# A Mamba-2 block with its MLP and a LoRA layer on one core: decay factors from broadcast cumulative sums in place of three f32 products

## The reference, cut to what matters

```
cs = cumsum(a)                                   # over the chunk's 128 tokens
Ldec[q, k] = exp(cs[q] - cs[k]) where k <= q, else 0
att = (C B^T) * Ldec ;  Yd = att @ (X * dt)
dec_end[k] = exp(cs[127] - cs[k])                # state handed to the next chunk
Yo = (C @ previous state) * exp(cs[q])
Y = Yd + Yo + D * X ;  y = Y * silu(z) ;  out = y @ w_out^T
```

## Time and profile before

| what | us |
|---|---|
| runs: median (lowest to highest), 3 runs | 778.89 (778.3 to 781.04) |
| the profiled execution, its own time | 783.21 |
| its span, first to last instruction | 781.5 |
| around the span | 1.7 |

### The profile page before, as it was taken

How to read it: one execution, slowest core, us unless ns; L and a number is a source line. 1 busy time by engine, 2 the same in 40 slices (tenths; PEclk the granted TensorE clock), 3 DMA queues, 4 the chain that set the end, 5 groups by cost and what they waited for, 6 DMA issues and landing times.

```text
span 781.5 us, 14105 instructions
## 1 busy us (share of the span) xinstructions
PE 746.2 (95%) x5626; PEld 533.6 (68%) x5634; DVE 513.3 (66%) x1181; ACT 342.5 (44%) x615; POOL 149.6 (19%) x201
## 2 busy tenths in 40 slices
PE   4999979989999999999999999999999999999985
PEld 3767846668666877588666877578666876667752
DVE  6798877787665757477664767467674767365356
ACT  2653766545623374235623363235633264222221
POOL 2220131105100321104200231103300241001021
PEclk8899999999999999999999999999999999999997
DMA  8970000030203120040202211050201201031001
GB/s 308 386 237 5 2 27 1 1 82 2 55 1 55 55 50 6 1 109 1 55 1 51 60 30 25 1 108 3 55 1 32 77 1 29 1 81 29 28 1 54
DMA packets 60082, 41.12 MB, mean 53 GB/s; under 512 B 45680, under 2 KB 45808, under 8 KB 60016
## 3 DMA queue, kind: packets, MB, share of 16 engines
q1 hardware_dynamic: 60016, 40.22, 18.6%
HBM read 25.01 MB, written 4.19 MB: 37 GB/s over the span
## 4 chain that ended last, share of the span: by engine, by line
PE 84%; DVE 8%; ACT 3%; DMA 2%; issue 1%; SPq 1%; POOL 0%; ACTq 0%; DVEq 0%
PE gu L1447 35%; PE wa L1447 24%; PE acc L1447 18%; PE wc L1447 6%; DVE xbc L1051 2%; DMA weights<-in_w_up 2%; DVE weights L973 2%; ACT weights L617 1%; DVE sg L1189 1%; DVE stats_a L1245 0%; DMA h2t<-xbc 0%; SPq L364 0%; DVE xbc L1177 0%; DVE hn L1251 0%; ACT sg L751 0%
## 5 line engine op out<-in xcount | busy, mean ns | idle before, releaser
L1447 PE MATMUL gu<-h2t,weights 128*128 128x256 f16 x2688 | 312.1, 273 | 1.9 <-DVE h2t L1183 1.0
L1447 PEld LDWEIGHTS gu<-h2t,weights 128*128 128x128 f16 x2688 | 261.9, 98 | 52.1 <-issue 10.3
L1447 PE MATMUL acc<-weights,act 128*128 128x512 f16 x672 | 163.4, 379 | 4.9 <-DVE act L1194 4.9
L1189 DVE SCALAR_TENSOR_TENSOR sg<-gu,bound,sg 128x256 f32<-128x256 f32 x112 | 53.2, 475 | 102.2 <-ACT sg L751 101.4
L751 ACT ACTIVATE sg<-gu,scale_inv 128x256 f32<-128x256 f32 x112 | 53.0, 473 | 146.5 <-PE gu L1447 146.3
L1447 PE MATMUL wa<-ht,weights 128*128 128x256 f16 x912 | 107.3, 275 | 1.3 <-DMA ht<-ra 1.1
L1447 PEld LDWEIGHTS acc<-weights,act 128*128 128x128 f16 x672 | 65.2, 98 | 62.2 <-DVE act L1194 6.9
L1447 PEld LDWEIGHTS wa<-ht,weights 128*128 128x128 f16 x912 | 90.0, 99 | 19.1 <-DMA ht<-ra 1.6
L761 ACT ACTIVATE act<-sg 128x256 f16<-128x256 f32 x112 | 46.6, 416 | 101.0 <-DVE sg L1189 101.0
L1194 DVE TENSOR_TENSOR act<-sg,act 128x256 f16<-128x256 f32 x112 | 49.8, 445 | 54.0 <-ACT act L761 54.0
L1051 DVE SCALAR_TENSOR_TENSOR xbc<-wa,conv_ws,xbc 128x253 f32<-128x253 f32 (+1 forms) x132 | 57.3, 476 | 1.8 <-ACT xbc L664 0.2
(11 more groups left out here) (233 smaller groups left out, 872.6 us busy)
## 6 DMA issues: line engine op xcount, KB each, us to landing
xa<-in_x SPq DMA_DIRECT2D x9, 512.0 KB, 3.6
weights<-in_x SPq DMA_DIRECT2D x7, 512.0 KB, 3.9
out_x<-h SPq DMA_DIRECT2D x14, 256.0 KB, 2.2
weights<-in_w_in SPq DMA_DIRECT2D x5, 512.0 KB, 6.5
weights<-in_w_down SPq DMA_DIRECT2D x3, 768.0 KB, 13.2
weights<-in_w_gate SPq DMA_DIRECT2D x2, 1024.0 KB, 13.6
weights<-in_w_up SPq DMA_DIRECT2D x2, 1024.0 KB, 14.0
weights<-in_w_gate SPq DMA_DIRECT2D x2, 768.0 KB, 14.4
```

The lines of the kernel that those rows point to most:

```text
L1189: nc.vector.scalar_tensor_tensor(sg[:, f % 2], GU[f % 2][:, SEQ:2 * SEQ], up_to_act, sg[:, f % 2], ALU.mult, ALU.mult).then_inc(sem("prod_ ...
L1447: return nc.tensor.matmul(dst, left, right, start=start, stop=stop)
```

## The change

Group 0 keeps the old way. For groups 1 to 7:

- GpSimd no longer spreads a_t over ra, TensorE no longer makes the three products.
- TensorE `a_cs`, at the end of slot 3: a_t (8 columns as the stationary side) by tri gives the cumulative sums as rows, [8, 128], and tri by a_t gives them as columns, [128, 8], both in the bank WC. ScalarE `a_cs` copies both to SBUF, in slot 3 ahead of the third Silu.
- SyncE `a_cs`, first in its step: eight DMAs, each reading one partition's row of 128 floats (512 bytes) 128 times and writing it to all partitions of ra.
- VectorE `a_fall`: for each chunk and head, a tensor_scalar that subtracts the column and takes the minimum with 0; chunk 0 in slot 4, behind a wait for all eight DMAs, chunk 1 in slot 5. The minimum bounds the entries above the diagonal, which the later product with tdt masks.
- ScalarE takes all three Exp in slot 5, in place (dec, and ra[:, 1] for ce).
- `a_h0` moves from slot 3 to slot 5, behind the second differences; SyncE's `a_x` moves behind `c_t3`. `a_state` moves from slot 6 to slot 7 on TensorE and ScalarE. TensorE's `c_logits` waits for the copied columns, because it writes the same bank.

```diff
+        cs_row = sb("cs_row", [TILES * H, P])
+        cs_col = sb("cs_col", [P, TILES, H])
...
+        cs_col_ps, cs_row_ps = WC[:, TILES * H:2 * TILES * H], WC[0:TILES * H, P:2 * P]
...
+            def a_cs(g):
+
+                sp.wait_ge(sem("cs_row_ready"), g)
+                for n in range(TILES * H):
+                    sp.dma_start(ra[:, n // H, n % H], cs_row[n:n + 1].unsqueeze(1).broadcast_to([1, P, P])).then_inc(cs_loaded, 16)
...
                 following = a is not None and a + 1 < GROUPS
-                if following:
-                    a_x(a + 1)
+                if a is not None:
+                    a_cs(a)
                 if c is not None and not alone(c):
                     c_t3(c)
                 if following:
+                    a_x(a + 1)
                     a_t1(a + 1)
...
                     a_xd(a)
-                    a_scan_in(a)
                     a_tdt(a)
...
+                eng.wait_ge(sem("fall_ready"), (g - 1) * TILES * H + H * (min(n, 1) + 1))
+                nc.scalar.activation(dst, dst, ACT.Exp).then_inc(sem("exp_ready"), 1)
+
+            def a_cs(g):
+
+                eng.wait_ge(sem("cs_ps_ready"), g)
+                nc.scalar.activation(cs_row[:], cs_row_ps, ACT.Copy).then_inc(sem("cs_row_ready"), 1)
+                nc.scalar.activation(cs_col[:].rearrange("p t h -> p (t h)"), cs_col_ps, ACT.Copy)\
+                    .then_inc(sem("cs_col_ready"), 1)
...
-                    3: lambda g: (a_silu(g, 2), a_z(g, 1)),
-                    4: lambda g: (a_tok(g), a_exp(g, 0), a_exp(g, 1)), 6: lambda g: (a_exp(g, 2), a_state(g)),
+                    3: lambda g: (a_cs(g), a_silu(g, 2), a_z(g, 1)), 4: lambda g: a_tok(g),
+                    5: lambda g: (a_exp(g, 0), a_exp(g, 1), a_exp(g, 2)), 7: lambda g: a_state(g),
...
+            def a_fall(g, j):
+
+                if j == 0:
+                    dve.wait_ge(cs_loaded, g * TILES * H * 16)
+                    dve.wait_ge(sem("cs_col_ready"), g)
+                    prev(g, 2, 2, dve, sem("y_ps_ready"))
+                for h in range(H):
+
+                    nc.vector.tensor_scalar(dec[:, j, h], ra[:, j, h], cs_col[:, j, h:h + 1], 0.0, ALU.subtract, ALU.min)\
+                        .then_inc(sem("fall_ready"), 1)
...
-                    2: lambda g: (a_conv(g, 2), a_dt(g)), 3: lambda g: a_h0(g),
-                    5: lambda g: (a_dec(g, 0), a_dec(g, 1), a_att(g, 0)), 6: lambda g: a_att(g, 1),
+                    2: lambda g: (a_conv(g, 2), a_dt(g)),
+                    4: lambda g: a_fall(g, 0), 5: lambda g: (a_fall(g, 1), a_h0(g), a_dec(g, 0), a_dec(g, 1), a_att(g, 0)), 6: lambda g: a_att(g, 1),
...
+            def a_cs(g):
+
+                pe.wait_ge(sem("a_ready"), g + 1)
+                a = a_t[:].rearrange("p t h -> p (t h)")
+                mm(cs_row_ps, a, tri[:], True, True)
+                mm(cs_col_ps, tri[:], a, True, True).then_inc(sem("cs_ps_ready"), 1)
...
-                    pe.wait_ge(sem("dtv_ready"), g + 3)
+                    pe.wait_ge(sem("cs_col_ready"), g + 2)
...
-                    3: lambda g: a_z(g, 1), 4: lambda g: (a_tok(g), a_dec(g, 0), a_dec(g, 1)),
-                    5: lambda g: (a_att(g, 0), a_dec(g, 2)), 6: lambda g: (a_att(g, 1), a_state(g)),
-                    7: lambda g: (a_y(g, 0), a_y(g, 1)), 8: lambda g: a_y_spread(g), 9: lambda g: a_o(g, 0),
+                    3: lambda g: (a_z(g, 1), a_cs(g)), 4: lambda g: a_tok(g),
+                    5: lambda g: a_att(g, 0), 6: lambda g: a_att(g, 1),
+                    7: lambda g: (a_state(g), a_y(g, 0), a_y(g, 1)), 8: lambda g: a_y_spread(g), 9: lambda g: a_o(g, 0),
```

More of the change, by code:

```diff
@@ L166, in build @@
         w0 = sb("w0", [P, H])
+        cs_row = sb("cs_row", [TILES * H, P])
+        cs_col = sb("cs_col", [P, TILES, H])
         tdt = hn[:].rearrange("p t (h q) -> p t h q", h=H)
         xw = hn[:, 0].rearrange("p (h q) -> p h q", h=H)
-        ce = hn[:, 1].rearrange("p (h q) -> p h q", h=H)
         y = sb("y", [P, H, SEQ])
@@ L289, in z_bank, with dec_bank @@
             return GU[b] if head(g) else bank(g, b)
-        def dec_bank(g, n):
-            return bank(g, [0, 1, 0][n])
+        def dec_bank(n):
+            return WA[[0, 1, 0][n]]
         def att_bank(g, j):
@@ L313, in ce_of @@
         def ce_of(g):
-            return first_ce if head(g) else ce
+            return first_ce if head(g) else ra[:, 1]
         def alone(g):
@@ L342, in build @@
         ht_loaded, h2t_loaded, h3t_loaded = sem("ht_loaded"), sem("h2t_loaded"), sem("h3t_loaded")
+        cs_loaded = sem("cs_loaded")
         masks_made = sem("masks_made")
@@ L485, in a_scan_in @@
             def a_scan_in(g):
-                pool.wait_ge(sem("a_ready"), g + 1)
+                pool.wait_ge(sem("a_ready"), 1)
                 for j in range(TILES):
-                    if j == 0:
-                        prev(g, 3, 3, pool, sem("dec_ps_ready"))
                     nc.gpsimd.tensor_tensor(ra[:, j], tri[:].unsqueeze(1).broadcast_to([P, H, P]),
@@ L494, in a_tdt @@
             def a_tdt(g):
+                pool.wait_ge(sem("a_ready"), g + 1)
                 for j in range(TILES):
@@ L640, in a_hi1 @@
                 eng.wait_ge(sem("rstd2_a_ready"), g + 1)
-                eng.wait_ge(sem("dec_ps_ready"), g * 3)
+                if head(g - 1):
+                    eng.wait_ge(sem("dec_ps_ready"), 3)
+                else:
+                    prev(g, 2, 2, eng, sem("y_ps_ready"))
                 if halved(g - 1):
@@ L655, in a_conv @@
                 if b == 0:
-                    prev(g, 3, 3, eng, sem("dec_ps_ready"))
                     prev(g, 2, 2, eng, sem("att_ps_ready"))
@@ L702, in a_exp @@
             def a_exp(g, n):
[L704 to L711, removed]
+                dst = (dec[:, n] if n < TILES else ce_of(g)).rearrange("p h q -> p (h q)")
+                if head(g):
+                    eng.wait_ge(sem("dec_ps_ready"), n + 1)
+                    nc.scalar.activation(dst, dec_bank(n)[:], ACT.Exp).then_inc(sem("exp_ready"), 1)
+                    return
+                eng.wait_ge(sem("fall_ready"), (g - 1) * TILES * H + H * (min(n, 1) + 1))
[5 more added lines that the diff above has]
+                    .then_inc(sem("cs_col_ready"), 1)
             def a_state(g):
@@ L1547, in flat, with a_dec @@
                 return t.rearrange("p h q -> p (h q)")
[L1549 to L1559, removed]
-                    .then_inc(sem("dec_ps_ready"), 1)
+            def a_dec(n):
+                pe.wait_ge(sem("exp_ready"), 1) if n == TILES else pe.wait_ge(sem("conv_in_ready"), 1 + n)
+                pe.wait_ge(sem("ra_ready"), min(n, 1) + 1)
+                mm(dec_bank(n)[:], (below if n < TILES else ones)[:], flat(ra[:, min(n, 1)]), True, True)\
+                    .then_inc(sem("dec_ps_ready"), 1)
+            def a_cs(g):
[3 more added lines that the diff above has]
+                mm(cs_col_ps, tri[:], a, True, True).then_inc(sem("cs_ps_ready"), 1)
             def a_att(g, j):
@@ L1565, in a_att @@
                     pe.wait_ge(sem("xbc_ready"), g * 3 + 3)
+                elif head(g):
+                    pe.wait_ge(sem("exp_ready"), 2)
                 else:
-                    pe.wait_ge(sem("exp_ready"), g * 3 + 2)
+                    pe.wait_ge(sem("sz_ready"), g * 2 + 2)
                 q = slice(j * P, j * P + P)
@@ L1769, in first @@
                 a_z(0, 0)
-                a_dec(0, 0)
-                a_dec(0, 1)
+                a_dec(0)
+                a_dec(1)
                 a_tok(0)
                 grams(GATE[1], UP[1])
-                a_dec(0, 2)
+                a_dec(2)
                 grams(GATE[2], UP[2])
```

## The result

| | before | after |
|---|---|---|
| median of the runs, us | 779.96 (778.3 to 783.67, 4 runs) | 887.16 (885.24 to 888.33, 4 runs) |
| the profiled execution: its own time, its span | 783.21, 781.5 | 888.33, 886.5 |
| mean granted clock | 0.984 | 0.930 |

The change makes the kernel slower: ratio 1.1365, 95% interval 1.1315 to 1.1414. The forecast was 772; rival 1, one narrow path for all eight rows, gave 899.

The account below looks back on a forecast made before the run. TensorE was taken as the bound, busy 746.2 us of 781.5. Gains of 3 us in step 1 and 3.9 in six steps, 6.9, gave 776.3 profiled, less 4.3 for the median: 772; range 764 to 900.

Parts of the forecast that it names:

- rival 1: SyncE's eight row DMAs: all read through one sixteenth of the DMA paths, 24 GB/s, about 120 us lost, 899; chance 0.34.
- The step that failed: SyncE's eight DMAs: issues from 458.7, 0.41 apart, last landing 2.1 after its issue, at L = 463.7.
- Break-even at 5.8 us after the first issue: Steps 2 to 7: the change gains only if the last row DMA lands (L) before 464.5, 5.8 us after first issue.
- slot 8 at L + 17.9: TensorE's slot 8 (a slot is one pass of f) begins 17.9 us after landing L or at 480.21, whichever is later.
- VectorE reaches the wait at 462.8: VectorE, after slot 4's gate product: arrives at its wait for the rows at 462.8 and waits 0.9 us.
- Removed 2.58 us of products: TensorE, groups 1 to 7: three f32 products of 512 columns go, 0.86 us each, 2.58 per group.
- Added 0.42: TensorE, slot 3: two small products for the sums, 0.22 and 0.20 us, together 0.42.
- Issues 0.41 apart: SyncE: the eight DMAs go out 0.41 us from issue to issue, 0.36 and a gap.
- Differences 0.20 from start to start: VectorE: eight 128 x 128 differences, 0.20 us from start to start, 0.8 for each tile of four.
- The y chain, the last product at L + 15.9: TensorE's last y product waits for the state's copy, starting 15.9 us after landing L; wait about 1.3 us a step.
- Step 1, 3 us less with a quick landing: Step 1: slot 8 begins at about 124 instead of 127.05, 3 us less; ends 0 and 5.
- The a_t wait, 2.2: Step 1: a_t is ready at 97.80, TensorE at 95.69, a new wait of 2.2 us.

Follow-up runs that it names:

- point 6: The change with rows spread by way of HBM, plus ScalarE's state copy ahead of its slot 7 activation copy: 766.35 against 781.65, ratio 0.9796.
- point 1: The change with its eight DMAs each reading all 128 partitions of a constant tile of ones instead of one partition: 787.24 against 781.48, ratio 1.007.
- point 5: The change with the eight DMAs replaced by a 4 KB store to HBM and one 512 KB broadcast load: 775.57 against 781.48, ratio 0.992.
- points 2 to 4: The change with rows on partitions 0, 4, ..., 28: 814.63; with alternating issue order: 829.25; with that order and second four rows on partitions 32 to 35: 889.13.
- points 2 and 3: The change with its eight rows on partitions 0, 4, ..., 28: 814.63; the change with DMAs issued in order 0, 4, 1, 5, 2, 6, 3, 7: 829.25.

## Why the prediction was wrong

The step that failed is "With 0.41 from issue to issue (0.36 and a gap) the last lands at 458.7 + 7 x 0.41 + 2.1 = 463.7", and its reason, "the store, like these, has whole rows and no transposing". It took the 2.1 us of a store that reads 128 partitions for a transfer that reads one. The earlier trace rows can't bear that, since every transfer in them is wide and the source's width is what bounds this one. Measured: 20.8 us after the first issue, not 5.0. Rival 1 named this mechanism, its place, and its price (23.3 us after the first issue, 105 us in six steps and 15 in step 1; measured 20.8, 89.0 and 13.9). It stood at 0.34 beside 0.31 for the forecast, but as one case against three that shared the wide source. By these chances rival 1 was the likeliest single case, though the text calls the forecast's the likeliest. That the range of 764 to 900 holds 887 is owed to rival 1 alone; the forecast, 7 us faster, had the wrong sign.

By its other steps:

- *Break-even at 5.8 us after the first issue, and slot 8 at L + 17.9*: right to 0.2. The table shows 17.5, and SyncE's first issue comes 0.2 later in its step than I had it: 88.88 - 65.4 (from slot 8 of the step before, 452.14, to 517.56) - 17.5 gives 6.0. The two misses offset each other in part. The step's loss by my 5.8 is 20.8 - 5.8 = 15.0, measured 14.8.
- *VectorE reaches the wait at 462.8, 4.1 us after the first issue*: 4.25 (521.81 against 517.56). The walk left out the 0.20 from a last product to the Silu. The waits read ahead of it were not placed rightly either: of the five for the activation two, not one, stand near the end (696.37 and 752.89). Nothing was worked out from that.
- *Removed 2.58 us of products*: right as far as can be seen. In point 6, where the landing costs nothing, a step is 1.81 us shorter, near the 2.58 - 0.65 = 1.93 left with the next figure. *Added 0.42*: measured 0.65 (from 516.44, where the z products give way, 2.62 after their start, to 517.09). The two groups start 0.31 and 0.25 apart, not 0.22 and 0.20, and 0.09 lies ahead of them.
- *Issues 0.41 apart*: 0.65 to 0.7 with a wide source, 2.0 once the queue is full. Mis-sized, and by itself enough to turn the gain into +0.5 a step (point 1).
- *Differences 0.20 from start to start*: right (four in 0.87, and h 0.78 after the first).
- *The y chain, the last product at L + 15.9*: L + 15.5 in point 5, with the wait where it was said to be. I expected 1.3 us a step from it, and it was 0.63: 0.4 because the chain is shorter, 0.2 because TensorE comes later behind its small products.
- *Step 1, 3 us less with a quick landing*: 131.63 against 134.88 in point 5, 3.3. *The a_t wait, 2.2*: 2.0.
- *Rival 1's size*: 899 against 887. Its 24 GB/s came from 385 GB/s over 16 engines, and 24 GB/s was measured in a window of nothing else; over the whole landing, 512 KB in 20.8 us, it is 25.2. L came 20.8 us after the first issue, not 23.3, and slot 8 0.4 sooner behind L. The Trainium skill's 27.6 GB/s for four partitions ("SBUF — State Buffer", "Door 1: The DMA port swizzle") gave 879: the measured time lies between the two. Its table of ports held where the runs could see it (points 2 to 4).
- *A granted clock that falls behind the waits*: seen, at half or little more from 534 to 548. It added next to nothing to the step: the slow products took the slack that TensorE has before the y chain. The y records of the change run in 2.12 us against 1.99 in point 6, so a wait of 0.1 is still in them (in steps 3, 4 and 6 one of 0.21 to 0.87), and slot 8 stays at L + 17.5.

What stays open: why neighbours in the queue overlap two or three deep and no more (points 2 and 3), why TensorE waits for h3's transposes in step 8, and whether a single DMA over all eight rows of SBUF would have landed sooner than eight; that was not tried.

## What to carry to other kernels

In these runs a DMA was as fast as its narrower side allowed: to spread rows from SBUF over all partitions, store them to HBM and load them from there with a broadcast (4.9 us for 512 KB in two issues, against 20.8 in eight), rather than read one partition 128 times. When the only durations at hand are of transfers of another width, ask what would bound this one, and give that case its full weight ahead of all the cases that share the assumption. In a step without slack, work out the landing at which a transfer breaks even before anything is built: the number here, 5.8 us, was good to 0.3 us over six landings from 4.9 to 21.3 us.

## What was not expected of the hardware

- The way by HBM: a 4 KB store issued at 541.04 had landed by 542.27, so the detour costs 1.2 us, less than a 256 KB store's 2.1.
- Overlap of DMAs on different ports goes by their order in the queue: rows 0 to 7 in order on two ports gave 25 GB/s, the same rows by turns 41 (512 KB in 12.7 us), eight ports 50 (in 10.5 us).
- With the source as the bound, the DMA engines still count as busy for 0.53 to 0.73 of the time, at 24 GB/s. The share has to be read beside the rate.
- The issue of one of these DMAs takes 0.49 us at the shortest and 2.0 at the median of the 56: the queue holds back SyncE, here up to 531.46. It cost nothing in this step: h3's transposes behind it were issued at 541.13, because VectorE makes their halves only behind its wait for the rows (from 540.36).
